# A fused attention and FP4 FFN kernel: FFN units moved beside the second batch, the first fills issued ahead, chunks begun two places later, the last group split

## The chip, the cores and the metric

The kernel runs on one core of one Trainium2 chip. The metric is the device time of one execution in microseconds. Three runs of the kernel before gave 1520.27, 1525.3 and 1527.58 us, median 1525.3. The profile is of one further execution.

## The reference, cut to what matters

```python
# x (8, 256, 512); 16 heads of 16 over C = 256 channels, T = 512 positions
Q, K, V = proj(Wq), proj(Wk), proj(Wv)
att = einsum('bhqd,bhkd->bhqk', Q, K) / sqrt(16) + b[0]
att = softmax(att * m + (1 - m) * NEG_INF)          # m: the mask over keys
y = einsum('bhqk,bhkd->bhqd', att, V) -> (8, 256, 512)
# FFN over the last axis, 512 -> 4096 -> 512, rows are the 2048 (batch, channel) pairs
Wg, Wu, Wd = dequant(4-bit codes, scales of blocks of 32)
out = x + (gelu_tanh(y @ Wg.T) * (y @ Wu.T)) @ Wd.T
```

## The kernel before, in words

**Attention.** Each of the 8 batches goes through four quads of heads. A quad has eight score steps (S00 to S31): two matmuls (line 852) into a pair of PSUM banks, then one exponential over 128 x 1024 on ScalarE (line 633). The product with V (line 866, A0 to A3), a copy (603), a transpose back (873, Y) and a normalisation on VectorE (712, 715, YN) follow, and GpSimd splits the result into two f16 parts y_hi and y_lo (lines 513 and 515). Beside this the maxima of the next quads are found: a step m is a matmul tile (line 836) and a reduction on VectorE, one tile at a time (line 693, batches 0 and 1) or a pair (line 700, later batches). Q, K and V of the next batch are projected in pieces (lines 812 and 822), stored to DRAM (369) and read back as stacks by ten DMAs for each half batch (fill_stack, lines 379 to 384, steps F0, F1 and G1).

**FFN.** The 2048 rows are four chunks of 512 (two batches each). For each chunk the 32 units of 128 hidden columns are gone through: gate (G0 to G3) and up (U0 to U3) are twelve matmuls of 512 columns each (lines 896 to 898, three products of f16 parts), gelu on ScalarE (608), the product inter on VectorE (748), its split into in_hi on ScalarE (615) and in_lo on GpSimd (527). After four units a group's down product (lines 944 to 946) is made for four row tiles r, twelve matmuls each, and VectorE adds it to acc (758).

**Weights.** In chunk 0 each unit's codes are decoded: VectorE unpacks (426, 428, 432), GpSimd multiplies by the scales (400), ScalarE makes the high half (409, weight_hi), VectorE the low half (414, weight_lo). The result is written to DRAM (345, spill_unit) and read again by the later chunks (352). The ring holds eight units. Units 0, 1 and 2 are decoded ahead of chunk 0.

**Order.** All engines walk the same list, written by `schedule()`. Batches below SOLO (0 and 1) use PLAN, with two pairs of score banks and no FFN work. Later batches use SHARED_PLAN, with one pair of score banks (the other two hold gate and up), in which a bar is a place where FFN steps are put: there are 16 in a quad, 64 in a batch. Chunk c begins after step YN of quad 0 of batch 2c + 2, which completes the y of its second batch, and its steps are spread evenly over the places up to the next chunk's start:

```python
ready = [n + 1 for n, (b, g, step, _) in enumerate(steps) if step == "YN" and g == 0 and b >= 2 and b % 2 == 0]
...
count = len(rest) // left
```

Gate of a chunk's first unit waits for y_lo of both batches (line 912). The queues run in order. SP begins with the loads of x[0] and wq, wk, wv, the loads of units 0 and 1 (576 KB each), then seed rows, the stores of Q and K, x[1] and the first fill. ScalarE's queue begins with the masks, among them a broadcast of seven batches' masks to 128 partitions (1.8 MB, line 583), from which VectorE finds any_key (line 723).

Of the kernel before, what the change touches and what calls it, by code (L numbers as in the profile page):

```python
# [6 lines left out]
P = 128  # L7
# [27 lines left out]
STEPS = CHUNKS * UNITS  # L35
# [3 lines left out]
LAST_CHUNK = (CHUNKS - 1) * UNITS  # L39
LAST_SHARED = LAST_CHUNK // GROUP - 1  # L40
SOLO = 2
# [6 lines left out]
def build(nc, x, mask, bias, wq, wk, wv, packed, scales, out):  # L48
# [3 lines left out]
    with ctx:  # L52
# [57 lines left out]
        mask_all = big[:, 0:B * T]  # L110
# [7 lines left out]
        seed = big[0:B, 5632:5632 + 768].bitcast(f16).rearrange("b (r t) -> b r t", r=3)  # L118
        seed_dram = nc.dram_tensor("seed_rows", [B, 3, T], f16, kind="Internal").ap()
# [15 lines left out]
        def out_bank(j, r):  # L135
# [7 lines left out]
        masks_in = sem("masks_in")  # L143
# [121 lines left out]
        def attention():  # L265
# [6 lines left out]
            for step in "| A2 | A3 | AO | | Y | YN".split():  # L272
                yield B, 0, step, None

        def ffn(c):

            for u in range(UNITS * c, UNITS * (c + 1)):
# [6 lines left out]
            if c == CHUNKS - 1:  # L284
                for step in ("G0", "G1"):
                    yield STEPS, step, None
                for r in range(4):
                    for i in range(GROUP):
                        yield STEPS, "D", (STEPS // GROUP - 1, r, i)

        def schedule():
# [3 lines left out]
            ready = [n + 1 for n, (b, g, step, _) in enumerate(steps) if step == "YN" and g == 0 and b >= 2 and b % 2 == 0]  # L295
            for b, g, step, arg in steps[:ready[0]]:
                yield "attention", b, g, step, arg
            for c in range(CHUNKS):
                rest = list(ffn(c))
                span = steps[ready[c]:ready[c + 1]] if c < CHUNKS - 1 else []  # L300
# [22 lines left out]
        def group_free(eng, n):  # L323


            wait_from(eng, sum_mm, 4 * (n // GROUP - 1))
# [20 lines left out]
        def reload_unit(sp, n):  # L347

            group_free(sp, n)
            if n < UNITS + RING:  # L350
# [690 lines left out]
```

## Time and profile before

| | |
|---|---|
| median of three runs | 1525.3 us |
| profiled execution, its time and its span | 1526.61 us, 1524.8 us |
| busy in the span: TensorE, VectorE, ScalarE, GpSimd | 1421.5, 698.3, 752.1, 309.6 us |
| an exponential, a table load, a weight_hi on ScalarE | 1.02, 1.28, 1.48 us |
| an L426 or L428 on VectorE while GpSimd is idle | 0.35 us |
| wait of TensorE for wk at the start | 2.1 us |

The table gives busy times of one execution. Busy time of TensorE is the union of its matmuls as the profile models them. The granted clock is a share of full speed, 1.0 for 2.4 GHz and 0.5 for 1.2 GHz.

### The profile page before, as it was taken

What the parts mean: (1) busy time and instruction counts of PE and PEld (TensorE: products, weight loads), DVE (VectorE), ACT (ScalarE), POOL (GpSimd) and SP (SyncE); (2) the same over time, 40 slices, a digit from 0 to 9 for tenths busy, and PEclk for the clock granted to TensorE, in tenths of its full rate; (3) what the DMA queues carried; (4) which work ended last, traced back from release to release, by engine and by line L of the source; (5) the groups of instructions that cost most, each with busy time, mean ns of one, the idle gap of its engine ahead of it and who ended that gap; (6) DMA issues with size and microseconds to landing.
All of it is one profiled execution on the core that took longest, in us unless ns stands there. A gap on an engine that the chain in (4) does not pass through costs nothing.

```text
span 1524.8 us, 18901 instructions
## 1 busy us (share of the span) xinstructions
PE 1421.5 (93%) x7376; PEld 555.1 (36%) x7376; DVE 698.3 (46%) x934; ACT 752.1 (49%) x855; POOL 309.6 (20%) x242
## 2 busy tenths in 40 slices
PE   3688779999999998999999998999999999999998
PEld 1122223333333333333433333333333334444443
DVE  5667668777778753433344333433343111111111
ACT  2255558666667663555665554556655631111110
POOL 3002024433444421111211111111111111111110
PEclk7589989999999999999999999999999999999999
DMA  5130324443354332432243320432222223233220
GB/s 182 51 87 15 101 78 163 154 131 122 108 183 157 133 125 65 143 99 84 84 128 106 101 84 20 155 119 83 84 84 83 84 83 138 83 126 123 83 84 28
DMA packets 51129, 157.91 MB, mean 104 GB/s; under 512 B 7632, under 2 KB 21072, under 8 KB 50912
## 3 DMA queue, kind: packets, MB, share of 16 engines
q1 hardware_dynamic: 48192, 153.80, 29.5%
q10 hardware_dynamic: 2848, 2.90, 0.6%
q8 instruction: 59, 0.97, 0.3%
q14 instruction: 30, 0.25, 0.1%
HBM read 118.64 MB, written 37.77 MB: 103 GB/s over the span
## 4 chain that ended last, share of the span: by engine, by line
PE 81%; DMA 4%; DVE 3%; ACT 3%; issue 3%; POOL 2%; SPq 2%; ACTq 1%; POOLq 0%; DVEq 0%
PE psum L896 14%; PE psum L897 13%; PE psum L898 13%; PE psum L944 8%; PE psum L945 7%; PE psum L946 7%; PE psum L866 7%; PE psum L852 4%; PE psum L836 4%; PE psum L812 2%; DMA wide<-seed_rows 2%; POOL dq_w L400 1%; DVE w_ring L414 1%; PE psum L822 1%; ACTq L393 1%
## 5 line engine op out<-in xcount | busy, mean ns | idle before, releaser
L633 ACT ACTIVATE big<-psum 128x1024 f32<-128x1024 f32 x256 | 260.1, 1024 | 328.4 <-PE psum L852 321.4
L896 PE MATMUL psum<-y_hi,w_ring 128*128 128x512 f16 x1024 | 390.5, 381 | 16.5 <-POOL y_lo L515 15.8
L898 PE MATMUL psum<-y_hi,w_ring 128*128 128x512 f16 x1024 | 389.6, 380 | 0.0
L897 PE MATMUL psum<-y_lo,w_ring 128*128 128x512 f16 x1024 | 389.4, 380 | 0.0
L700 DVE TENSOR_REDUCE maxima<-psum 128x2 f32<-128x1024 f32 x179 | 219.2, 1225 | 253.6 <-PE psum L836 253.3
L527 POOL TENSOR_TENSOR in_lo<-inter,in_hi 128x512 f16<-128x512 f32 x128 | 150.4, 1175 | 811.1 <-ACT in_hi L615 810.5
L748 DVE SCALAR_TENSOR_TENSOR inter<-psum,gelu 128x512 f32<-128x512 f32 x128 | 88.2, 689 | 315.4 <-PE psum L898 301.4
L944 PE MATMUL psum<-w_ring,in_hi 128*128 128x512 f16 x512 | 195.5, 382 | 7.7 <-ACT gelu L608 4.3
L945 PE MATMUL psum<-w_ring,in_hi 128*128 128x512 f16 x512 | 194.8, 380 | 0.0
L946 PE MATMUL psum<-w_ring,in_lo 128*128 128x512 f16 x512 | 194.6, 380 | 0.0
L896 PEld LDWEIGHTS psum<-y_hi,w_ring 128*128 128x128 f16 x1024 | 100.1, 98 | 202.6 <-issue 82.7
L836 PE MATMUL psum<-wide 51*128 51x512 f16 x512 | 129.0, 408 | 46.4 <-DMA wide<-seed_rows 32.7
L615 ACT CAST in_hi<-inter 128x512 f16<-128x512 f32 x128 | 78.7, 615 | 178.5 <-DVE inter L748 178.4
L758 DVE SCALAR_TENSOR_TENSOR acc<-psum,acc 128x512 f32<-128x512 f32 x128 | 88.5, 691 | 166.0 <-PE psum L946 165.4
L866 PE MATMUL psum<-big,wide 128*32 128x512 f32 x1024 | 140.9, 623 | 7.7 <-DVE y_f L715 6.5
L898 PEld LDWEIGHTS psum<-y_hi,w_ring 128*128 128x128 f16 x1024 | 100.5, 98 | 121.6 <-issue 1.3
L608 ACT ACTIVATE gelu<-psum 128x512 f32<-128x512 f32 x128 | 76.4, 597 | 131.1 <-PE psum L898 130.0
L897 PEld LDWEIGHTS psum<-y_lo,w_ring 128*128 128x128 f16 x1024 | 100.5, 98 | 102.1 <-issue 0.8
L633 ACT ACT_TABLE_LOAD x93 | 119.3, 1283 | 29.9 <-issue 28.6
L400 POOL TENSOR_TENSOR dq_w<-dq_code,dq_scales 128x1536 f32<-128x1536 f16 x32 | 99.8, 3118 | 147.9 <-DVE w_ring L414 122.7
L693 DVE TENSOR_REDUCE maxima<-psum 128x1 f32<-128x512 f32 x154 | 99.5, 685 | 50.4 <-PE psum L836 48.3
L852 PE MATMUL psum<-wide 53*128 53x512 f16 x512 | 111.9, 404 | 10.4 <-DMA wide<-max_lo 8.0
(69 smaller groups left out, 987.3 us busy)
## 6 DMA issues: line engine op xcount, KB each, us to landing
w_ring<-w_parts SPq DMA_DIRECT2D x96, 768.0 KB, 7.2
w_parts<-w_ring SPq DMA_DIRECT2D x32, 768.0 KB, 3.3
dq_scales<-scales SPq DMA_DIRECT2D x32, 384.0 KB
wide<-qk_parts SPq DMA_DIRECT2D x64, 128.0 KB
qk_parts<-wide SPq DMA_DIRECT2D x60, 128.0 KB
dq_packed<-packed SPq DMA_DIRECT2D x32, 192.0 KB
small<-x SPq DMA_DIRECT2D x8, 512.0 KB, 6.6
wide<-qk_parts SPq DMA_DIRECT2D x64, 64.0 KB
```

The lines of the kernel that those rows point to most:

```text
L527: nc.gpsimd.tensor_tensor(in_lo[:, u % IN_RING, :], inter[:, :], in_hi[:, u % IN_RING, :], ALU.subtract).then_inc(in_lo_s, 1)
L633: nc.scalar.activation(p_exp[:, k, :, i], p_score[:, bank:bank + 2, :], ACT.Exp, scale=SCORE_SCALE).then_inc(exp_done, 1)
L700: nc.vector.reduce_max(maxima[:, g % 2, n // 2:n // 2 + 9:8], p_max, AX.X).then_inc(max_red, 2)
L836: nc.tensor.matmul(p_max[:, n % 2, :], q_stack[rows, side, s, t * P:(t + 1) * P], k_stack[rows, side, s, :], start=True, stop=True).then_i ...
L852: last = nc.tensor.matmul(p_score[:, bank + e, :], k_stack[rows, side, s, k * P:(k + 1) * P], q_stack[rows, side, s, :], start=True, stop= ...
L866: last = nc.tensor.matmul(p_av[r:r + 32, :], v_rows[:, k, head_of(g, e, i), :], p_exp[:, k, e, i, :], start=(k == 0), stop=(k == TT - 1))
L896: nc.tensor.matmul(dst, w[:, 0, k % 2, cols], hi, start=(k == 0), stop=False)
L897: nc.tensor.matmul(dst, w[:, 0, k % 2, cols], lo, start=False, stop=False)
L898: return nc.tensor.matmul(dst, w[:, 1, k % 2, cols], hi, start=False, stop=(k == TT - 1))
L944: nc.tensor.matmul(dst, in_hi[:, s, rows], w_hi, start=(i == 0), stop=False)
L945: nc.tensor.matmul(dst, in_hi[:, s, rows], w_lo, start=False, stop=False)
L946: last = nc.tensor.matmul(dst, in_lo[:, s, rows], w_hi, start=False, stop=(i == GROUP - 1))
```

## The change

Visits take the place of units: a visit is a unit, a chunk and a range of the chunk's 512 columns. Units 0 to 7 are first visited with columns 0 to 255 of chunk 0 (batch 0's rows), a segment of its own that begins at batch 1's YN. The second segment holds units 8 to 31 with all 512 columns and then units 0 to 7 again with columns 256 to 511; their weights are read back from DRAM. Matmuls, gelu, inter, in_hi and in_lo of such a visit are 256 wide, and its groups have two row tiles. SOLO goes from 2 to 1, so batch 1 uses SHARED_PLAN, and units 0, 1 and 2 are all decoded in batch 0's plan. The first stack fill is issued before x[1] and the unit loads, the broadcast of seven masks is replaced by a small store and a broadcast of eight numbers. A segment begins at the second place after YN. The down product of the very last group goes unit by unit over the four row tiles.

```diff
+EARLY = 8
+VISITS = ([(n, 0, 0, 256) for n in range(EARLY)] + [(n, 0, 0, 512) for n in range(EARLY, UNITS)]
+          + [(n, 0, 256, 512) for n in range(EARLY)]
+          + [(n, c, 0, 512) for c in range(1, CHUNKS) for n in range(UNITS)])
+STEPS = len(VISITS)
+SEGMENTS = [0, EARLY] + [UNITS * c + EARLY for c in range(1, CHUNKS)] + [STEPS]
+ROWS = [range(VISITS[s][2] // P, VISITS[s][3] // P) for s in range(0, STEPS, 4)]
-SOLO = 2
+SOLO = 1
...
-            "F1 A2 m A3 m AO m S00 S01 V1a m m S10 V1b V1h m S11 m Y S20 MT MH XH YN m m ML S21 MV A0 m m A1 m "
-            "S30 m S31 m Q0a m Q0b m Q0h Q0l",
-            "X A2 m S00 m d0 K0a K0b m K0h S01 m S10 m A3 K0l AO m m S11 Y m MT MH ML S20 MV m S21 m Q1a YN m Q1b "
-            "Q1h m S30 Q1l A0 m m A1 m S31 m",
+            "F1 A2 m A3 m AO m S00 S01 V1a d00 m d01 m d02 S10 V1b V1h m S11 m Y S20 MT MH XH YN m h0 m ML S21 MV A0 l0 m m A1 m "
+            "S30 m S31 m Q0a m Q0b m Q0h Q0l L2",
+            "X A2 m S00 m d10 K0a K0b m K0h S01 d11 m S10 m A3 K0l AO m m S11 Y m MT MH ML S20 MV m S21 m Q1a YN m Q1b "
+            "Q1h m S30 Q1l A0 m d12 m A1 m S31 m",
...
-            for step in "| A2 | A3 | AO | | Y | YN".split():
+            for step in "| A2 | A3 | AO | | Y | YN | |".split():
...
-                for r in range(4):
-                    for i in range(GROUP):
+                for i in range(GROUP):
+                    for r in ROWS[-1]:
                         yield STEPS, "D", (STEPS // GROUP - 1, r, i)
...
+            ready = []
+            for n, (b, g, step, _) in enumerate(steps):
+                if step == "YN" and g == 0 and (b == 1 or b >= 2 and b % 2 == 0):
+                    places = [m for m in range(n, len(steps)) if steps[m][2] == "|"]
+                    ready.append(places[1] + 1)
...
-            load_unit(sp, 0)
-            load_unit(sp, 1)
+            sp.wait_ge(dve_own, 2)
+            sp.dma_start(any_dram, any_b).then_inc(any_out, 16)
             sp.wait_ge(setup, 4)
             sp.wait_ge(fixed, 2)
             sp.dma_start(seed_dram, seed).then_inc(seed_out, 16)
             store_qk(sp, 0, 0, 0)
             store_qk(sp, 0, 0, 1)
+            sp.wait_ge(seed_out, 16)
+            fill_stack(sp, 0, 0, 0, False)
             sp.wait_ge(x_lo_s, 1)
             sp.wait_ge(v_proj, 1)
             load_x(sp, 1)
-            sp.wait_ge(seed_out, 16)
-            fill_stack(sp, 0, 0, 0, False)
+            sp.wait_ge(any_out, 16)
+            sp.dma_start(any_key[:, :], any_dram.rearrange("b o -> (b o)").partition_broadcast(P)).then_inc(any_in, 16)
+            load_unit(sp, 0)
+            load_unit(sp, 1)
             move_max(sp, 0, 0, 0)
...
-            act.dma_start(mask_all[:, T:],
-                          mask[1:].rearrange("b t -> (b t)").partition_broadcast(P)).then_inc(masks_in, 16)
...
-            for n in range(8):
-                reduce_maximum(0, 0, n)
-            weight_lo(dve, 0)
-            for n in range(8, 16):
+            for n in range(16):
                 reduce_maximum(0, 0, n)
...
-                w, c = w_ring[:, u % RING], u // UNITS % 2
+                _, c, first, end = VISITS[u]
+                w, dst = w_ring[:, u % RING], dst[:, first:end]
...
+                u, n = GROUP * j + i, r - ROWS[j][0]
+                if n == 0:
+                    pe.wait_ge(in_lo_s, u + 1)
                 if i == 0:
-                    if r == 0:
-                        pe.wait_ge(in_lo_s, GROUP * j + GROUP)
```

## Rows read from the trace of the kernel before

**Rows 1.** The page: busy time, and the span in 40 slices.

```profile
PE 1421.5 (93%) x7376; PEld 555.1 (36%) x7376; DVE 698.3 (46%) x934; ACT 752.1 (49%) x855; POOL 309.6 (20%) x242
...
PE   3688779999999998999999998999999999999998
...
PEclk7589989999999999999999999999999999999999
```

**Rows 2.** Windows: length, busy us of each engine, granted clock, DMA share, GB/s.

```profile
61.35:138.75 77.40, 60.46 (x346) 16.87 (x345) 49.80 (x86) 39.97 (x48) 8.45 (x8) 0.82 0.24 64
138.75:207.90 69.15, 54.19 (x338) 16.69 (x342) 49.92 (x88) 40.28 (x48) 9.46 (x10) 0.91 0.32 88
...
207.90:221.80 13.90, 7.59 (x58) 3.04 (x51) 8.99 (x12) 5.13 (x7) 3.26 (x3) 0.75 0.14 57
...
371.30:551.30 180.00, 170.60 (x915) 66.36 (x908) 137.70 (x173) 120.79 (x127) 75.89 (x41) 1.00 0.40 135
```

**Rows 3.** Waits of TensorE over the whole span: us, times, longest.

```profile
PE psum L836 <- DMA wide<-seed_rows: 32.7, 4, 17.9
PE psum L896 <- POOL y_lo L515: 15.8, 4, 4.8
```

**Rows 4.** Timeline, start and length: batch 1's start, and the four chunks' first matmuls.

```profile
138.75 0.15 DVE L774 COPY any_now<-any_key 128x1 f32<-128x1 f32 x1
...
221.76 0.61 PE L896 MATMUL psum<-y_hi,w_ring 128*128 128x512 f16 x1 [4.75 <-POOL y_lo L515]
...
576.85 0.39 PE L896 MATMUL psum<-y_hi,w_ring 128*128 128x512 f16 x1 [4.15 <-POOL y_lo L515]
...
924.72 0.39 PE L896 MATMUL psum<-y_hi,w_ring 128*128 128x512 f16 x1 [4.15 <-POOL y_lo L515]
...
1257.87 0.39 PE L896 MATMUL psum<-y_hi,w_ring 128*128 128x512 f16 x1 [2.74 <-POOL y_lo L515]
```

**Rows 5.** Chain and timeline of the first 110 us: start, length, what.

```profile
1.75 11.77 DMA big<-wk
...
26.32 0.40 SPq L333 DMA_DIRECT2D small<-x  x1
...
31.41 0.30 SPq L384 DMA_DIRECT2D wide<-seed_rows  x1
...
40.34 0.61 PE L836 MATMUL psum<-wide 51*128 51x512 f16 x2 [17.89 <-DMA wide<-seed_rows]
...
48.78 1.20 PE L836 MATMUL psum<-wide 51*128 51x512 f16 x2 [1.66 <-DVE maxima L693]
...
102.80 6.53 DMA wide<-seed_rows
```

**Rows 6.** VectorE's groups within batch 3 (371 to 551 us): busy, mean ns, idle before.

```profile
L700 DVE TENSOR_REDUCE maxima<-psum 128x2 f32<-128x1024 f32 x32 | 39.1, 1221 | 10.6 <-PE psum L836 10.4
L414 DVE SCALAR_TENSOR_TENSOR w_ring<-dq_w,w_ring 128x1536 f16<-128x1536 f32 x16 | 28.0, 1751 | 0.0
L428 DVE TENSOR_SCALAR dq_sign<-dq_packed 128x384 uint32<-128x384 uint32 x30 | 19.9, 662 | 0.0
L426 DVE TENSOR_SCALAR dq_code<-dq_packed 128x384 uint32<-128x384 uint32 x30 | 17.1, 569 | 11.0 <-POOL dq_w L400 11.0
L432 DVE TENSOR_TENSOR dq_code<-dq_sign,dq_code 128x768 uint32<-128x768 uint32 x16 | 15.3, 958 | 0.5
```

**Rows 7.** The chain, V's projection of batch 2: start, length.

```profile
193.38 0.78 PE psum L822 x12
```

**Rows 8.** SP's queue: the writing out of units 0, 1 and 2.

```profile
196.67 11.68 SPq L345 DMA_DIRECT2D w_parts<-w_ring  x3
```

**Rows 9.** Timeline of the end: the last group's first matmul and two adds.

```profile
1509.40 0.58 PE L944 MATMUL psum<-w_ring,in_hi 128*128 128x512 f16 x1 [2.72 <-POOL in_lo L527]
...
1516.48 0.69 DVE L758 SCALAR_TENSOR_TENSOR acc<-psum,acc 128x512 f32<-128x512 f32 x1 [1.90 <-PE psum L946]
...
1519.07 0.69 DVE L758 SCALAR_TENSOR_TENSOR acc<-psum,acc 128x512 f32<-128x512 f32 x1 [1.90 <-PE psum L946]
```

More of the change, by code:

```diff
@@ L34 @@
 CHUNKS = B * C // 512
-STEPS = CHUNKS * UNITS
+EARLY = 8
[5 more added lines that the diff above has]
+ROWS = [range(VISITS[s][2] // P, VISITS[s][3] // P) for s in range(0, STEPS, 4)]
+ADD_ORDER = [(j, r) for j, rows in enumerate(ROWS) for r in rows]
+ADD_NO = {key: n + 1 for n, key in enumerate(ADD_ORDER)}
 RING = 2 * GROUP
@@ L294, in schedule @@
             steps = list(attention())
-            ready = [n + 1 for n, (b, g, step, _) in enumerate(steps) if step == "YN" and g == 0 and b >= 2 and b % 2 == 0]
+            ready = []
[3 more added lines that the diff above has]
+                    ready.append(places[1] + 1)
             for b, g, step, arg in steps[:ready[0]]:
                 yield "attention", b, g, step, arg
-            for c in range(CHUNKS):
+            for c in range(len(SEGMENTS) - 1):
                 rest = list(ffn(c))
-                span = steps[ready[c]:ready[c + 1]] if c < CHUNKS - 1 else []
+                span = steps[ready[c]:ready[c + 1]] if c + 1 < len(ready) else []
                 left = sum(step == "|" for _, _, step, _ in span)
@@ L457, in _ @@
                 if kind == "ffn":
-                    u, c = b, b // UNITS
+                    u = b
+                    c = VISITS[u][1] if u < STEPS else CHUNKS
                     if step == "G0" and u < STEPS:
@@ L596, in _ @@
             store_qk(act, 0, 1, 1)
-            weight_hi(act, 0)
             max_part(0, 0, True)
@@ L649, in _ @@
                     x_high(b + 1)
-                elif step == "wh" and b < SOLO:
-                    weight_hi(act, b + 1)
+                elif step in ("h0", "h1", "h2") and b < SOLO:
+                    weight_hi(act, int(step[1]))
         @block.vector
@@ L747, in inter_part @@
                 wait_from(dve, in_lo_s, u)
-                nc.vector.scalar_tensor_tensor(out=inter[:, :], in0=up_bank(u),
+                cols = slice(*VISITS[u][2:])
+                nc.vector.scalar_tensor_tensor(out=inter[:, cols], in0=up_bank(u)[:, cols],
                                                scalar=I_SCALE / (Y_SCALE * W_SCALE),
-                                               in1=gelu[:, u % 2, :], op0=ALU.mult, op1=ALU.mult).then_inc(inter_s, 1)
+                                               in1=gelu[:, u % 2, cols], op0=ALU.mult, op1=ALU.mult).then_inc(inter_s, 1)
             def add_rows(j, r):
-                dve.wait_ge(sum_mm, 4 * j + r + 1)
-                if j % (UNITS // GROUP) == 0:
-                    dve.wait_ge(acc_in, 16 * (j // (UNITS // GROUP)) + 16)
+                dve.wait_ge(sum_mm, ADD_NO[j, r])
+                c = VISITS[GROUP * j][1]
+                earlier = [ADD_NO[m, r] for m in range(j) if VISITS[GROUP * m][1] == c and r in ROWS[m]]
+                if earlier:
+                    dve.wait_ge(acc_add, earlier[-1])
                 else:
-                    dve.wait_ge(acc_add, 4 * (j - 1) + r + 1)
+                    dve.wait_ge(acc_in, 16 * c + 16)
                 nc.vector.scalar_tensor_tensor(out=acc[:, r, :], in0=out_bank(j, r), scalar=1.0 / (I_SCALE * W_SCALE),
@@ L786, in _ @@
                 elif step[0] == "d" and b < SOLO:
-                    decode(dve, b + 1, int(step[1]))
-                elif step == "wl" and b < SOLO:
-                    weight_lo(dve, b + 1)
+                    decode(dve, int(step[1]), int(step[2]))
+                elif step in ("l0", "l1", "l2") and b < SOLO:
+                    weight_lo(dve, int(step[1]))
         @block.tensor
@@ L891, in three_products @@
             def three_products(dst, u, cols, k):
-                w, c = w_ring[:, u % RING], u // UNITS % 2
+                _, c, first, end = VISITS[u]
+                w, dst = w_ring[:, u % RING], dst[:, first:end]
                 cols = slice(cols + k // 2 * P, cols + k // 2 * P + P)
-                hi, lo = (y[:, k, 512 * c:512 * c + 512] for y in (y_hi, y_lo))
+                hi, lo = (y[:, k, 512 * (c % 2) + first:512 * (c % 2) + end] for y in (y_hi, y_lo))
                 nc.tensor.matmul(dst, w[:, 0, k % 2, cols], hi, start=(k == 0), stop=False)
```

92 lines of the change are left out of this document (47 added, 45 removed), and 8 rows, old and new, of the table PLAN.

## The prediction

> **What bounds the kernel now.** I read the page first, then a table of windows, then TensorE's waits, and then the order of time at the two ends. TensorE is busy 93% of the span, and the next engine 49% [rows 1]. The 40 slices show where the other 7% and most of the lost speed lie: the digits of PE are 3, 6, 8, 8, 7 in the first five slices (38 us each) and 9 almost everywhere after that, and the clock row has its low digits there too [rows 1]. The windows say the same in us: batch 0's attention works TensorE 60.5 of 77.4 us at a granted clock of 0.82, batch 1's 54.2 of 69.2 at 0.91, the start of batch 2 7.6 of 13.9 at 0.75, while batch 3, which has FFN units beside it, works it 170.6 of 180.0 at 1.00 [rows 2]. So up to 221.8 us the chain is attention's own (DMA landings, reductions, exponentials), and behind that it is the sum of TensorE's work.
>
> Two prices follow. The last row tiles end 2.59 us apart, 12 matmuls each [rows 9]: 0.216 us for a matmul of 512 columns, 36 of them or 7.77 us for a unit, 248.7 us for a chunk. Chunk 1 begins at 576.85 and chunk 2 at 924.72 [rows 4]: 347.9 us, less the 4.15 us wait at its end 343.7, less 248.7 leaves 95.0, so 47.5 us for one batch of attention and, with 64 places in a batch, 0.74 us of it a place. Chunk 0 took 355.1 us (221.76 to 576.85), 7.2 more.
>
> TensorE's own waits add up to few things: 32.7 us for stacks that land and 15.8 us for y_lo at the four chunk starts [rows 3].
>
> **First fills.** Before, the first stack fill stands in SP's queue behind the load of x[1], which is issued at 26.32 because it waits for x_lo; the last of its ten DMAs goes out at 31.41 and TensorE begins at 40.34, after 17.9 us of waiting [rows 5]. After, the fill stands behind the four stores of Q and K alone. Those waited for K's split; K's matmuls waited for wk, which took 11.8 us from its issue [rows 5] in the company of 1.8 MB of broadcast masks and 1.1 MB of unit loads, both of which go away or go later. I put K's split 2 us earlier (TensorE idled 2.1 us for wk, by the table above), at 15.8; two store issues of 0.6 us each, a landing that I put at 2 to 5 us, ten fill issues as before in 4.9 us, then 6.5 us (the later fill) to 8.9 us (this one) to the first matmul [rows 5]: 30.6 to 35.6. I take 33.3, which is 7 us earlier; bounds 3 and 10. Besides, weight_lo of unit 0 no longer stands between the first sixteen reductions: TensorE waited 1.66 us for it [rows 5]. Start: -8.7 us.
>
> On the queues the trace shows only that big<-wk took 11.8 us while everything else was in flight. The Trainium skill, "DMA: Bandwidth & Descriptors", section "Issuing engines are not separate DMA queues", says that transfers issued by SP and by ACT run on the same sixteen engines; by it the masks on ACT's queue did delay wk, and by the opposite only the unit loads behind wk could have, and the 2 us would be nearer nothing. The trace does not decide it.
>
> **Batch 0.** It now holds the decoding of three units where it held one (unit 0's was in the preamble). One unit costs VectorE two L426, two L428, L432 and L414. Beside attention alone that is 0.35 x 4 (the table above) + 0.96 + 1.75 [rows 6] = 4.1 us, so +8.3 us, and +3.0 us on ScalarE. VectorE is busy 49.8 of these 77.4 us [rows 2] and half of its slack lies between reductions that TensorE waits for in turn. I take half: +4, bounds 0 and +8.3.
>
> **Batch 1 with eight units beside it.** Before, from batch 1's start (138.75) to chunk 0's first matmul (221.76) [rows 4]: 83.0 us. Batch 1 now uses the plan of batches 2 to 7, with one pair of score banks. Its opening up to YN should be like that of batch 2: 13.9 us from batch start to y ready [rows 2]; the two places later fit into what was the 4.75 us wait [rows 4]. Then a batch's length of 64 places with 72 FFN steps, one a place, two in the last eight.
>
> TensorE's work there is 47.5 + 8 x 24 x 0.108 = 20.7 + group 0's two row tiles 5.2 = 73.4 us. VectorE's: 32 pair reductions 39.1; eight decodings at the lengths they have beside GpSimd, 2 x 0.57 + 2 x 0.66 + 0.96 + 1.75 = 5.2, so 41.3 [rows 6]; eight half-width inter at about 0.38, 3.0; two adds 1.4; the remaining pieces of a batch 6.7 (138.75 to 207.9 less reductions and weights): 91.5 us. ScalarE's, by the lengths in the table above: 32 exponentials 32.8, sixteen table loads 20.5, eight weight_hi 11.9, some 14 of small ones: 79 us. VectorE is the longest, so 91.5 is the floor. In-order queues add to it. A unit has four score steps, two places each. Between the first two pairs VectorE has a reduction and four decode pieces, 3.7 us; between the next two a reduction, L432 and weight_lo, 3.9; in the other two it has little, and TensorE's 2.3 us (1.49 attention, 0.65 FFN, 0.16 down) or the exponential's chain rule; I put 2.5 there. 3.7 + 3.9 + 2.5 + 2.5 = 12.6, times 8 = 101 us. Upper bound: batch 1 alone took 69.2 us on 49.9 of VectorE [rows 2], a ratio of 1.38, so 126; this holds 11.3 us of DMA waits that the shared plan should not have.
>
> So 13.9 + 101 = 114.9, +31.9 against 83.0; of this 25.9 us is FFN work that need not be done later, and 2 x 0.74 = 1.5 is batch 2's attention of the two places. Net +4.5, bounds -5 and +29.5.
>
> Is a matmul of 256 columns really half? None is in the trace. Below it, V's projection has twelve of 128 columns, each with its own weights, in 0.78 us or 0.065 each [rows 7]; above it, 512 cost 0.216. So 0.108, with 0.065 and 0.216 as ends; the upper end for 384 such matmuls would cost 41 us, but the 128-column rows exclude it, since they have as many loads and less cover. The Trainium skill, "TensorE: Matmul & The Clock Gate", section "LDWEIGHTS (loading the stationary operand)", has a load cost of columns / 1.2, 107 ns for 128 columns; as a floor for each pair that would leave 256 columns at 0.108 too. Rows 7 go below that floor, so the trace does not bear it out as one.
>
> **Rest of chunk 0.** The restart at 221.76 was cold (a matmul of 0.61 us against 0.39 at the next chunk [rows 4]) and cost about 2; TensorE now comes working. 21 of 29 decodings remain in it: -1. The eight half units at its end have 2.9 steps a place: gelu waits for a table load 1.28, an exponential 1.02 and itself 0.3, 2.6 us, covered by four up steps (1.3) and 1.4 places (1.0): 0.3 to 0.4 us a unit, +3; bounds 0 and +8. Sum 0. The eight further reloads of 768 KB run beside 0.2 to 0.4 of DMA load [rows 2], and three units ahead: nothing; without that cover a reload is 7.2 us.
>
> **Chunks two places later.** The waits at 576.85, 924.72 and 1257.87 were 4.15, 4.15 and 2.74 [rows 4]. Two places hold score and reduction work of 1.5 us and two shares of the previous chunk's FFN (3.9 us each), over 9 us in all. The last chunk too keeps two places. -11.0.
>
> **Last group split.** TensorE stood 2.72 us until in_lo at 1509.40 and began again at half speed (0.58 us for a matmul) [rows 9]. Now 36 of 48 matmuls need only older units and begin where up ends, 1509.40 - 2.72 = 1506.7; 48 x 0.216 = 10.4 ends at 1517.1, against 1521.6 (the last add comes one interval after 1519.07). All four adds and 256 KB stores now come within 2 us, where the last store had the DMA engines to itself: +0.8. -3.7.
>
> Sum: -8.7 + 4 + 4.5 + 0 - 11.0 - 3.7 = -14.9. The profiled execution took 1526.6 us for its span of 1524.8; the median is 1525.3. From the median: 1510.4, rounded 1510.
>
> **Rivals.**
> (A) The eight units drag batch 1. One pair of score banks makes TensorE wait for every exponential, and VectorE's decoding delays each pair reduction, so the stretch takes 126 us as bounded: 1535, slower. It decides from 116 us on (no gain left) and is measurably slower from 124. For it: VectorE would be 91.5 of 101, denser than the 137.7 of 180 of batch 3 [rows 2]. Against: batch 3 shows that decoding and shared banks cost TensorE only 9 us in 180 where work fills in. 0.17.
> (B) The start stays. The first fill's landing, not its place in the queue, is the length, and x and wq are no sooner: 1510 + 7 = 1517. For it: 8.9 us of the 17.9 were landing. 0.12.
> (C) Slack takes it all: batch 0 absorbs the decoding (-4), the stretch runs at VectorE's floor (-9.5), half units don't stall (-3): about 1494. For it: 27.6 us in which VectorE is idle in batch 0 [rows 2]. 0.16.
> (D) The split of the chunk does nothing because batch 1's fills for batch 2 stand behind spills in SP's queue, three of which took 11.7 us to issue [rows 8], and the gaps move to batch 2: +10, 1520. 0.05.
> The forecast itself has 0.5, with 1502 to 1518 as its own range.
>
> **Numbers.** 1510 us, 80% range 1494 to 1531. A change below 0.5% (7.6 us) is about what this measurement can't tell from none. Faster by more: the forecast but for its edge (0.45), C (0.16), half of B (0.05): 0.66. Within: the rest of these, D and a third of A: 0.19. Slower: 0.15.
>
> **What would show it.** In the new profile: the first L836 at 33 and not 40; batch 1's start near 134; first half-width matmul about 14 us later and the first full chunk work near 249; no L896 wait for y_lo; half-width matmuls 0.11 apart; VectorE over 80% busy between; the last down matmuls straight behind the last up. What would make it wrong: above all the length between units 0 and 8.

## The result, and the profile after

The changed kernel took 1542.0 us (median of four runs, 1536.5 to 1543.0) against 1524.3 us for the kernel before, run beside it: a ratio of 1.0106, 95% interval 1.0074 to 1.0138. It is slower by some 16 us; the prediction had 15 us faster. The profiled executions are closer: 1536.5 us for a span of 1534.6 (the fastest of the four), against a span of 1524.8. So the ledger below has 9.8 us to explain against the 14.9 us gain that was forecast, 24.7 us apart.

The page of the changed kernel: busy time, and the first lines of the span in 40 slices (38 us each).

```profile
PE 1423.8 (93%) x7568; PEld 569.3 (37%) x7568; DVE 680.1 (44%) x909; ACT 777.0 (51%) x887; POOL 317.3 (21%) x250
...
PE   3777888898989998999999999999999999999999
...
PEclk7688899999999999999999999999999999999999
```

Against [rows 1] the engines are as busy as before (TensorE 1423.8 for 1421.5), and the clock is below 9 in the first five slices where it was in the first three and the sixth. What is new is 8s in place of 9s in slices 7, 8, 10 and 12, where attention and FFN already run together. (The 8 in slice 16 was there before.)

Windows of the changed kernel: batch 0; batch 1 up to batch 2's start; first half-width matmul to first full-width one; from there to chunk 1. The columns are as in [rows 2].

```profile
53.49:129.67 76.18, 58.42 (x329) 16.15 (x329) 56.84 (x97) 42.24 (x49) 14.65 (x10) 0.85 0.31 80
129.67:226.96 97.29, 79.15 (x513) 30.28 (x511) 68.57 (x92) 64.92 (x75) 26.21 (x20) 0.88 0.40 122
143.96:248.15 104.19, 83.84 (x564) 34.78 (x565) 75.76 (x103) 74.84 (x85) 33.67 (x24) 0.89 0.46 147
248.15:603.35 355.20, 320.36 (x1801) 130.54 (x1799) 217.76 (x286) 225.78 (x244) 121.36 (x72) 0.98 0.38 128
```

The timeline at those places: start, length, what, and in brackets the wait before it.

```profile
24.54 0.32 SPq L400 DMA_DIRECT2D wide<-seed_rows  x1
...
33.77 0.61 PE L851 MATMUL psum<-wide 51*128 51x512 f16 x2 [15.48 <-DMA wide<-seed_rows]
...
143.96 0.39 PE L912 MATMUL psum<-y_hi,w_ring 128*128 128x256 f16 x1 [1.13 <-POOL y_lo L536]
...
151.91 0.27 PE L913 MATMUL psum<-y_lo,w_ring 128*128 128x256 f16 x1
152.02 0.27 PE L914 MATMUL psum<-y_hi,w_ring 128*128 128x256 f16 x1
...
248.15 0.64 PE L912 MATMUL psum<-y_hi,w_ring 128*128 128x512 f16 x1
...
603.35 0.39 PE L912 MATMUL psum<-y_hi,w_ring 128*128 128x512 f16 x1 [1.05 <-POOL y_lo L536]
```

From these starts and those of [rows 2, 4, 5, 9], stage by stage:

| stretch | before | after | difference | predicted |
|---|---|---|---|---|
| up to batch 0's start | 61.35 | 53.49 | -7.9 | -8.7 |
| batch 0 | 77.4 | 76.2 | -1.2 | +4 |
| batch 1's start to first full-width matmul of a chunk | 83.0 | 118.5 | +35.5 | +31.9 |
| from there to chunk 1 | 355.1 | 355.2 | +0.1 | -24.9 |
| chunks 1 to 3 and the end | | | -16.7 | -17.2 |

The prediction gave the two last lines in one sum, -42.1. I divide it by where the work lies. Gate and up of eight half units (20.7) and chunk 1's wait (4.15) leave the fourth line. The half group's down product (5.2) falls in chunk 1, and with it the other waits (6.9), the 1.5 us of attention and the split group (3.7) go into the fifth line.

The fourth line is the surprise. That stretch has lost 20.7 us of TensorE's FFN work and 3.1 us of wait at its end, and is as long as before. Its attention is the same, because its start and its end both moved by two places. Its window in the kernel before (that of the changed kernel is the last one above):

```profile
221.76:576.85 355.09, 336.65 (x1800) 129.51 (x1801) 258.62 (x330) 238.14 (x251) 140.94 (x79) 0.99 0.40 137
```

TensorE is busy 320.4 us for 336.7, which is 16.3 less and not 20.7, at a granted clock of 0.98 for 0.99, and idle 34.8 us for 18.4.

The first line's mechanism is there (the stack fill's last DMA is issued at 24.54 where it was 31.41), and so are the chunks' two places (the y_lo waits are nearly gone) and the split group (13.6 us from the last up-product's reader to the end instead of 18.0).

TensorE's waits over the whole span of the changed kernel: us, times, longest.

```profile
PE psum L867 <- ACT big L654: 23.7, 16, 3.6
PE psum L851 <- DMA wide<-seed_rows: 19.6, 2, 15.5
...
PE psum L912 <- POOL y_lo L536: 2.2, 2, 1.1
```

And between 248 and 603 us alone, the stretch that did not shrink:

```profile
PE psum L851 <- DVE maxima L721: 9.7, 5, 4.0
PE psum L881 <- DVE y_f L736: 9.6, 7, 1.9
PE psum L912 <- ACT gelu L627: 7.3, 5, 2.6
PE psum L961 <- DVE inter L761: 5.1, 4, 1.9
```

y_lo has gone from 15.8 us [rows 3] to 2.2. Of the waits for exponentials (big), 15.4 us lie beside the half-width units. In the stretch there are 31.7 us of waits for maxima, y_f, gelu and inter. (y_f is the normalised attention output; the next quad's product with V writes the bank that it is read from, and so waits for it.) The kernel before has three like them, over its whole span:

```profile
PE psum L866 <- DVE y_f L715: 6.5, 6, 1.1
PE psum L944 <- ACT gelu L608: 4.3, 6, 0.7
PE psum L836 <- DVE maxima L700: 1.2, 1, 1.2
```

That is some 20 us more of waits.

### The profile page after: what moved, and what is told of

Read it like the earlier page. It is cut to its first block, busy times and chain, and to the rows that moved or that the text cites. A ratio compares the mean times of both kernels' runs of the same rounds, so it can differ in the third digit from the quotient of the medians.

```text
span 1534.6 us, 19370 instructions
## 1 busy us (share of the span) xinstructions
PE 1423.8 (93%) x7568; PEld 569.3 (37%) x7568; DVE 680.1 (44%) x909; ACT 777.0 (51%) x887; POOL 317.3 (21%) x250
## 4 chain that ended last, share of the span: by engine, by line
PE 72%; DVE 7%; ACT 6%; DMA 5%; issue 4%; SPq 2%; POOL 2%; ACTq 0%; DVEq 0%; POOLq 0%
PE psum L912 12%; PE psum L914 11%; PE psum L913 11%; PE psum L961 7%; PE psum L963 7%; PE psum L962 7%; PE psum L881 7%; PE psum L867 3%; PE psum L851 3%; DMA dq_scales<-scales 3%; PE psum L827 2%; DVE maxima L721 2%; DVE w_ring L430 2%; POOL dq_w L416 2%; ACT big L654 2%
## 5 line engine op out<-in xcount | busy, mean ns | idle before, releaser
L912 PE MATMUL psum<-y_hi,w_ring 128*128 128x512 f16 (+1 forms) x1088 | 403.4, 371 | 12.7 <-ACT gelu L627 10.5
L913 PE MATMUL psum<-y_lo,w_ring 128*128 128x512 f16 (+1 forms) x1088 | 401.9, 369 | 0.0
L914 PE MATMUL psum<-y_hi,w_ring 128*128 128x512 f16 (+1 forms) x1088 | 401.8, 369 | 0.0
L721 DVE TENSOR_REDUCE maxima<-psum 128x2 f32<-128x1024 f32 x211 | 258.3, 1224 | 231.3 <-PE psum L851 230.5
L548 POOL TENSOR_TENSOR in_lo<-inter,in_hi 128x512 f16<-128x512 f32 (+1 forms) x136 | 149.9, 1102 | 917.5 <-ACT in_hi L636 917.3
L761 DVE SCALAR_TENSOR_TENSOR inter<-psum,gelu 128x512 f32<-128x512 f32 (+1 forms) x136 | 89.4, 657 | 320.1 <-PE psum L914 301.9
L912 PEld LDWEIGHTS psum<-y_hi,w_ring 128*128 128x128 f16 x1088 | 106.6, 98 | 213.3 <-issue 114.7
L636 ACT CAST in_hi<-inter 128x512 f16<-128x512 f32 (+1 forms) x136 | 80.2, 590 | 199.7 <-DVE inter L761 197.8
L881 PE MATMUL psum<-big,wide 128*32 128x512 f32 x1024 | 144.7, 638 | 14.3 <-DVE y_f L736 14.1
L851 PE MATMUL psum<-wide 51*128 51x512 f16 x512 | 119.9, 402 | 39.2 <-DMA wide<-seed_rows 19.6
L914 PEld LDWEIGHTS psum<-y_hi,w_ring 128*128 128x128 f16 x1088 | 107.2, 99 | 116.2 <-issue 1.4
L627 ACT ACTIVATE gelu<-psum 128x512 f32<-128x512 f32 (+1 forms) x136 | 77.8, 572 | 132.3 <-PE psum L914 131.2
L913 PEld LDWEIGHTS psum<-y_lo,w_ring 128*128 128x128 f16 x1088 | 107.1, 98 | 96.4 <-issue 1.6
L627 ACT ACT_TABLE_LOAD x102 | 130.9, 1283 | 1.8
L654 ACT ACT_TABLE_LOAD x101 | 129.6, 1283 | 1.8
```

The lines of the kernel that those rows point to most:

```text
L627: nc.scalar.activation(gelu[:, u % 2, cols], gate_bank(u)[:, cols], ACT.Gelu_apprx_tanh, scale=1.0 / (Y_SCALE * W_SCALE)).then_inc(gelu_s, 1)
L654: nc.scalar.activation(p_exp[:, k, :, i], p_score[:, bank:bank + 2, :], ACT.Exp, scale=SCORE_SCALE).then_inc(exp_done, 1)
L721: nc.vector.reduce_max(maxima[:, g % 2, n // 2:n // 2 + 9:8], p_max, AX.X).then_inc(max_red, 2)
L851: nc.tensor.matmul(p_max[:, n % 2, :], q_stack[rows, side, s, t * P:(t + 1) * P], k_stack[rows, side, s, :], start=True, stop=True).then_i ...
L881: last = nc.tensor.matmul(p_av[r:r + 32, :], v_rows[:, k, head_of(g, e, i), :], p_exp[:, k, e, i, :], start=(k == 0), stop=(k == TT - 1))
L912: nc.tensor.matmul(dst, w[:, 0, k % 2, cols], hi, start=(k == 0), stop=False)
```

## The experiments

Chunk 0 is measured the same way in all of them: from VectorE's first reading of a full-width up product (unit 0's, or unit 8's where there are half-width visits) to chunk 1's first.

**1. No units beside batch 1, and 2. no later places.** The first keeps everything of the change but the eight half-width visits; units 0 to 2 are still decoded in batch 0. The second keeps those visits, and starts every chunk at YN. The diffs are cut to the lines that matter, here and below.

```diff
 e1
-EARLY = 8
-VISITS = ([(n, 0, 0, 256) for n in range(EARLY)] + [(n, 0, 0, 512) for n in range(EARLY, UNITS)]
...
+VISITS = [(n, c, 0, 512) for c in range(CHUNKS) for n in range(UNITS)]
+SEGMENTS = [UNITS * c for c in range(CHUNKS + 1)]
-SOLO = 1
+SOLO = 2
...
 e2
-            for step in "| A2 | A3 | AO | | Y | YN | |".split():
+            for step in "| A2 | A3 | AO | | Y | YN".split():
...
-                    places = [m for m in range(n, len(steps)) if steps[m][2] == "|"]
-                    ready.append(places[1] + 1)
+                    ready.append(n + 1)
```

> The changed kernel without its first part: 32 full units for chunk 0, begun beside batch 2, batch 1 in the plan with two pairs of score banks; early fills, the two later places and the split last group stay. The stages of the changed kernel say: start -8 us, chunk starts -11, tail -4.5, and the loss lies between batch 1's start and chunk 1. Theory A (the two later places, not the eight units, spoil the rest of chunk 0 by moving FFN steps against the attention steps): chunk 0 takes 25 us or more over the 343.7 of its work here too, and the median is 1525 to 1535. Theory B (the loss comes from the eight half-width visits themselves and what they shift): chunk 0 takes 355 or less as before and the median is 1500 to 1506.

> The changed kernel with every segment begun at YN as before, all else as changed. Theory A (phase): the stretch from unit 8's first gate to chunk 1 falls from 355 to 330 us or less, the three chunk starts wait 4.15, 4.15 and 2.7 us again, median 1515 to 1525. Theory B (the half-width visits themselves): the stretch stays at 350 to 360 and the waits at the chunk starts come back, median 1548 to 1554.

The first took 1528.5 us, ratio 1.0018 (1.0003 to 1.0033): the later places, early fills and split group together, forecast at some -20, gave nothing. Chunk 0 lasted 372.6 us where before it was 354.0, chunk 1's start wait included. The second took 1533.6 us, 1.0047 (1.0032 to 1.0062); units 8 onward lasted 347.6 us from the first gate to chunk 1's, of which 6.5 us are chunk 1's start wait: between what the two theories gave. So each of the two edits makes this stretch longer.

**3. Neither: only early fills and the split group.** Both edits above in one kernel.

> Early fills and the split last group alone: no half-width visits, segments begun at YN. By the stages of the changed kernel -8 (start), 0 to -1 (batch 0, which now decodes three units), -4.5 (tail): median 1510 to 1514, chunk 0 in 352 to 358 us. Both theories expect the same; it is the fourth cell of the table, and it shows whether decoding unit 2 in batch 0 instead of batch 1 frees time there (up to -5).

1516.3 us, ratio 0.9934 (0.9919 to 0.9948). Start and end are worth 9 us by the medians, a little less than expected, and chunk 0 is 357.0. The waits beside batch 2's last two quads differ between this kernel and that of experiment 1. The timeline of the kernel of experiment 1:

```profile
293.20 0.38 PE L909 MATMUL psum<-y_hi,w_ring 128*128 128x512 f16 x1 [1.70 <-ACT gelu L624]
...
299.32 1.06 PE L878 MATMUL psum<-big,wide 128*32 128x512 f32 x8 [1.64 <-DVE y_f L733]
...
339.70 0.38 PE L909 MATMUL psum<-y_hi,w_ring 128*128 128x512 f16 x1 [1.21 <-ACT gelu L624]
...
346.26 1.06 PE L878 MATMUL psum<-big,wide 128*32 128x512 f32 x8 [2.08 <-DVE y_f L733]
```

And that of experiment 3:

```profile
296.69 1.07 PE L877 MATMUL psum<-big,wide 128*32 128x512 f32 x8 [1.08 <-DVE y_f L732]
...
301.82 0.38 PE L957 MATMUL psum<-w_ring,in_hi 128*128 128x512 f16 x1 [0.72 <-ACT gelu L623]
...
341.73 1.06 PE L877 MATMUL psum<-big,wide 128*32 128x512 f32 x8 [1.08 <-DVE y_f L732]
...
346.87 0.38 PE L957 MATMUL psum<-w_ring,in_hi 128*128 128x512 f16 x1 [0.73 <-ACT gelu L623]
```

The same places wait in one quad and the next, 47 us apart in the kernel of experiment 1 and 45 in that of experiment 3: a periodic pattern, with another price in each kernel. What makes it periodic stands in the code. After the first places a chunk issues three FFN steps a place, four units with their down product are 4 x 8 + 16 = 48 steps, and a quad is 16 places: 48 again. So FFN and attention meet in the same way in every quad. Which FFN step has just been issued at a named attention step, such as YN, I call the alignment.

**4. Loads behind the spill.** In the changed kernel the scales of three units come late. The trace's chain there (start, length, what):

```profile
338.88 0.30 SPq L400
...
339.63 10.93 DMA dq_scales<-scales
...
350.58 0.04 DVE dq_code L442
```

SP issues a ten-DMA fill up to 339.2 and a unit's codes and scales right behind it, the scales at 339.63. They land after 10.9 us, and VectorE, which decodes them, has waited 7.1. VectorE's waits between 248 and 603 us in the changed kernel:

```profile
DVE dq_code L442 <- DMA dq_scales<-scales: 18.9, 3, 7.1
```

```diff
                     if step == "G0" and u < STEPS:
-                        if u + AHEAD_UNITS + 1 < UNITS:
-                            load_unit(sp, u + AHEAD_UNITS + 1)
+                        if u == 0:
+                            load_unit(sp, AHEAD_UNITS + 1)
...
                             spill_unit(sp, n)
+                        if u + AHEAD_UNITS + 2 < UNITS:
+                            load_unit(sp, u + AHEAD_UNITS + 2)
```

> The changed kernel with one order in SP's queue altered: the load of a unit's codes and scales is issued right behind the spill before it, so that no fill of ten DMAs can stand between. Theory A1 (VectorE waits for late scales three times, 5.9, 7.1 and 5.9 us, because the load stands behind a fill, and the max tiles, inter and normalisation queue up behind it): the three waits go and 15 to 25 us with them, median 1517 to 1527. Theory A2 (the late scales are hidden; it is the order of steps within VectorE's queue that makes TensorE wait for y_f, inter and gelu): at most 5 us, median 1537 to 1542.

1534.1 us, 1.0051 (1.0036 to 1.0067), between the two. The waits for scales are gone, and 8 us by the medians with them; chunk 0 fell by 6.4 us, from 354.3 to 347.9. TensorE's waits for y_f and gelu stayed. So the late scales were a part of the loss, not its cause.

**5 to 7. Where chunk 0 starts.** On experiment 1, chunk 0 alone begins at YN, or five or eight places later.

```diff
+                    later = {2: 0}.get(b, 2)          # e6: 5, e7: 8
-                    ready.append(places[1] + 1)
+                    ready.append(places[later - 1] + 1 if later else n + 1)
```

> Early fills, split last group, and the two later places for chunks 1, 2 and 3 only; chunk 0 begins at YN of batch 2, no half-width visits. Theory A (a group of four units with its down product is 48 steps, at three steps a place sixteen places, which is one quad; so the point at which chunk 0 begins sets, for all eight quads, where decoding falls against YN, and two places later is a bad coincidence): chunk 0 takes 357 us from first inter to first inter as with all chunks at YN, and chunks 1 and 2 keep their gain of 2.9 and 2.2 us: span 1508 to 1511, median 1510 to 1513. Rival C (the loss of 15.6 us has to do with where chunk 0 ends, two places inside batch 4's first quad, beside chunk 1's start): 372 us as with all chunks two places later, median 1523 to 1528.

> As the run before, but chunk 0 begins five places after YN. Theory A: the cost of chunk 0 depends on the place within the quad and not on the delay as such; so it may be above or below 372, and TensorE's waits of 0.6 us and more in chunk 0 recur at the same places of each quad, some 47 us apart, at other steps than with 0 or 2 places. Rival D (each place later costs chunk 0 some 8 us because work beside attention is lost): 390 us or more.

> As before, chunk 0 eight places after YN. Theory A: again a length of its own between 350 and 380 us, periodic waits. Rival D: over 400 us.

Start at YN: 1523.4 us, 0.9984 (0.9966 to 1.0002), chunk 0 367.0 us, with the waits of experiment 1 from the second quad on. Five places later (one execution): chunk 0 370.6 us, the same waits. So the start does not set the pattern; the chunk's end does. The code says why: `count = len(rest) // left` gives two steps a place to the first 16 or so places and then exactly three, counted back from the last place. Moving the end of chunk 0 two places later (chunk 1's start) therefore moves every FFN step of batches 2 and 3 by six steps against attention. Eight places later (one execution), the number of places is small enough for the surplus to fall otherwise, so that the steps stand eight behind instead of six: 359.6 us, although the same work is pressed into fewer places. Rival D, which had 390 us or more and over 400 us for the two, is out.

**8. Thin decoding.** On experiment 1, five decode operations of units 3 to 31 work on 48 of 384 columns.

```diff
+            e = WORDS // 2 if n < AHEAD_UNITS else WORDS // 16
...
-                nc.vector.tensor_tensor(dq_code[:, :, :], dq_sign[:, :, :], dq_code[:, :, :],
+                nc.vector.tensor_tensor(dq_code[:, :, 0:e], dq_sign[:, :, 0:e], dq_code[:, :, 0:e],
```

> No half-width visits, all chunks two places later (as the first experiment), but for units 3 to 31 the five decoding instructions on VectorE work on 48 of 384 columns each, so most of those weights are stale; everything else, its waits too, is in place. Theory A with VectorE's decoding as what collides (normalisation and inter stand behind it in VectorE's queue): the 372.6 us of chunk 0 fall to 350 or less and the waits for y_f and gelu shrink below 5 us together. Rival E (the collision is on ScalarE: weight_hi and table loads before gelu; VectorE is only along for it): waits of gate and down for gelu stay above 10 us, chunk 0 at 362 to 372.

Chunk 0 fell by 13 us to 359.6 (one execution, span 1513.8), between theory A and rival E; y_f's waits fell from 13.7 to 9.8, while those of gate's matmuls for gelu stayed at 9.5, with the same 1.70 and 1.21 in the same places. TensorE's idle time gives 4.9 of the 13 us (27.1 for 32.0). The other 8.1 are its matmuls, busy 332.5 us for 340.6, at a granted clock of 1.00 for 0.98. So VectorE's decoding is a part, and the waits for gelu are another. What stands before such a wait in ScalarE's order its timeline in experiment 1 shows; no run tried it alone:

```profile
285.85 0.62 ACT L633 CAST in_hi<-inter 128x512 f16<-128x512 f32 x1 [3.05 <-DVE inter L758]
...
286.87 0.58 ACT L618 COPY av_sb<-psum 128x512 f32<-128x512 f32 x1
287.46 1.28 ACT L651 ACT_TABLE_LOAD   x1
288.75 1.02 ACT L651 ACTIVATE big<-psum 128x1024 f32<-128x1024 f32 x1
289.67 1.48 ACT L422 ACTIVATE w_ring<-dq_w 128x1536 f16<-128x1536 f32 x1
291.17 1.28 ACT L624 ACT_TABLE_LOAD   x1
292.46 0.60 ACT L624 ACTIVATE gelu<-psum 128x512 f32<-128x512 f32 x1
```

Here ScalarE works without a pause for 7.2 us, from inter's split to the end of the gelu for which gate's matmul at 293.20 (above) waits.

**9, 11, 12. The alignment alone.** On experiment 1 (no half-width visits, two places later), chunk 0's steps are shifted against attention and the rest is left as it is.

```diff
-                    count = len(rest) // left
+                    count = (len(rest) - -6 * (c == 0 and left > 8)) // left      (e9; e11 has -12, e12 has 8)
```

> As the first experiment (no half-width visits, all chunks two places later), but chunk 0's steps are handed out six ahead, up to eight places before its end, so that at every YN of batches 2 and 3 the same FFN step has just been issued as in the kernel before (the last up step of a group's fourth unit) and not six steps less. Theory A': FFN steps go at exactly three a place counted back from the chunk's end, so the end sets the alignment in every quad; with the old alignment chunk 0 takes 355 to 359 us from first inter to first inter instead of 372.6, TensorE waits under 2 us a quad, and the gain at the chunk starts stays: span 1508 to 1512. Rival C' (the two more places at the end cost by themselves, whatever the alignment): 367 to 373 us, span 1520 to 1527.

> As the first of these, but twelve steps ahead, which is six more than in the kernel before: an alignment that none of the kernels had. Theory A': a length of chunk 0 of its own between 350 and 375 us with waits that recur once a quad. The rival that delay as such costs: below the 357 of the old alignment, since FFN steps come sooner.

> No half-width visits, chunk 0's steps handed out eight later still: at every YN of batches 2 and 3 the same step as in the changed kernel (second gate step of a group's third unit). Theory A': chunk 0 takes 375 to 392 us, with the changed kernel's waits once a quad (y_f, max tiles, inter) and VectorE waiting 4 us or more for scales that landed late behind a stack fill. Rival B': nothing like the changed kernel's waits without its half-width visits, 360 to 373 us, no late scales.

With the old alignment back: **1505.2 us (1499.1 to 1508.5), ratio 0.9846 (0.9804 to 0.9888)**, faster than both kernels, chunk 0 349.1 us. Against experiment 1 only the order of the same steps differs, and 23.5 us of chunk 0 go. TensorE's waits from 210 to 575 us in it:

```profile
PE psum L878 <- DVE y_f L733: 8.1, 8, 1.1
PE psum L958 <- ACT gelu L624: 4.3, 6, 0.7
PE psum L909 <- POOL y_lo L533: 2.0, 1, 2.0
PE psum L848 <- DVE maxima L718: 1.2, 1, 1.2
```

Six steps ahead (experiment 11, one execution, 1521.1 us) chunk 0 took 368.4 us. Fourteen steps behind is the alignment that the changed kernel has. Without half-width visits, one execution with it took 1538.8 us, span 1536.9, chunk 0 381.6 us. Its waits from 210 to 600 us are for the same four things as the changed kernel's:

```profile
PE psum L878 <- DVE y_f L733: 13.2, 8, 3.1
PE psum L848 <- DVE maxima L718: 12.8, 8, 4.8
PE psum L909 <- ACT gelu L624: 7.4, 4, 2.6
PE psum L958 <- DVE inter L758: 4.1, 4, 1.2
```

Its timeline shows the late scales too, and a matmul that waits for the reduction behind them:

```profile
461.33 0.36 DVE L439 TENSOR_SCALAR dq_code<-dq_packed 128x384 uint32<-128x384 uint32 x1 [7.70 <-DMA dq_scales<-scales]
...
463.15 0.61 PE L848 MATMUL psum<-wide 51*128 51x512 f16 x2 [3.98 <-DVE maxima L718]
```

Batch 3 lies wholly inside chunk 0, with 64 places and 192 FFN steps in every one of these kernels, so its length can be compared without a correction. Its windows in experiments 9 and 12 (columns as in [rows 2]):

```profile
361.63:541.67 180.04, 170.66 (x915) 66.38 (x908) 137.72 (x174) 120.84 (x127) 75.87 (x41) 1.00 0.40 135
365.68:569.52 203.84, 180.28 (x926) 68.62 (x924) 135.19 (x179) 122.22 (x127) 82.37 (x42) 0.96 0.36 122
```

Of the 23.8 us between them, 14.2 are idle time of TensorE (23.6 for 9.4). The other 9.6 are the same matmuls taking longer, at a granted clock of 0.96 for 1.00. Over the whole of chunk 0 it is 20.7 of idle time and 11.8 of slower matmuls. So a worse alignment comes with a second price beside the waits; that the waits bring the clock down is not shown apart.

**10. The old alignment in the changed kernel.** All of the change stays; the second segment's steps run 14 ahead until ten places before its end.

```diff
+                    count = (len(rest) - -14 * (c == 1 and left > 10)) // left
```

> The changed kernel, complete, with the steps of the segment of units 8 to 31 handed out fourteen ahead until ten places before its end, which gives the alignment of the kernel before. Theory A': of the 355 us from unit 8's first gate to chunk 1 some 20 us go, no late scales, span 1511 to 1517. Rival B' (the eight half-width visits cost by themselves, in that segment too): 345 to 355 us stay, span 1526 to 1535.

1519.2 us, ratio 0.9946 (0.9921 to 0.9971); chunk 0 from unit 8 took 333.1 us instead of 354.3, with no late scales. So 21 us of the change's loss are alignment (15.7 of idle time, 5.5 of slower matmuls), and with it undone the change gains 0.5%. It still lies 14 us above experiment 9.

**13 and 14. What the units beside batch 1 cost.** Experiment 9 with batch 1 on the shared plan but no FFN in it, and experiment 10 with four visits.

```diff
 e13, on e9
-SOLO = 2
+SOLO = 1
 e14, on the changed kernel
-EARLY = 8
+EARLY = 4
+                    count = (len(rest) - -6 * (c == 1 and left > 10)) // left
```

> The fastest version so far (early fills, later places, old alignment, split last group, no half-width visits), but batch 1 goes in the plan with one pair of score banks, without any FFN work or decoding beside it. Batch 1 took 65.6 us from its start to batch 2's start there, and 97.6 with the plan and the eight half-width visits. Theory P (the plan itself costs: every score step waits for the exponential before it): 85 to 95 us here, span 1520 to 1530. Theory V (VectorE's decoding of eight units and the table loads beside it cost): 66 to 75 us, span 1502 to 1511.

> The changed kernel with the old alignment for the second segment, but four half-width visits beside batch 1 instead of eight. Theory P: nearly the whole price is paid for half the work moved: batch 1 at 88 to 96 us, span 1514 to 1520. Theory V: half the price, batch 1 at 80 to 84 us, span 1508 to 1512.

One execution each, spans 1506.9 and 1509.6. Batch 1 took 65.6 us in experiment 9, 75.2 in 13, 81.8 in 14 and 97.6 in 10, so theory V is nearer than P in both. TensorE's longest waits in experiment 13 from 131 to 200 us, and in experiment 10 from its first half-width matmul (147.3) to 248 us:

```profile
PE psum L864 <- ACT big L651: 12.0, 10, 3.6
```

```profile
PE psum L867 <- ACT big L654: 17.5, 11, 2.7
```

Against experiment 9's span of 1501.8 the three are 5.1, 7.8 and 17.7 us longer. But up to batch 1's start all four run the same code, and four executions of experiment 9 lie 9.4 us apart. Counted from batch 1's start to the end, the plan alone costs 4.1 us (1375.5 for 1371.4), four visits 7.2 (1378.6) and eight 15.4 (1386.8). With single executions the first two are not clear of noise. Work is moved forward into batch 1, but there it takes more than it saves.

The table has the kernels by how far their FFN steps stand from those of the kernel before at each quad's YN in batches 2 and 3 (from chunk 0's second quad on), and the length of chunk 0 in us. Kernels whose chunks start at YN have chunk 1's start wait in it (before, e3, e2). Experiments 4 and 8, with the loads or the decoding changed, and 14, with four visits, are left out:

| steps | full-width chunk 0 | with half-width visits |
|---|---|---|
| 0 | before 354.0, e3 357.0, e9 349.1, e13 349.1 | e10 333.1 |
| 6 ahead | e11 368.4 | |
| 6 behind | e1 372.6, e5 367.0, e6 370.6 | |
| 8 behind | e7 359.6 | e2 347.8 |
| 14 behind | e12 381.6 | after 354.3 |

## Why the prediction was wrong, point by point

**Start, -8.7:** right, -7.9. Both parts came: the first maximum at 33.77 where 33 was named, and no wait for unit 0's weight_lo. Rival B, in which the start stays, is out, and wk was not waited for at all: its load took 6.6 us where it took 11.8 [rows 5]. Masks and unit loads both went from beside it, so which of them delayed it is not shown. (The terms behind 33 add up to 30.4 to 35.8, not 30.6 to 35.6; it changes nothing.)

**Batch 0, +4:** -1.2. Its slack took the decoding; here rival C was nearer (no cost at all). One trace can't say more: in the fifteen traces of kernels with this batch 0 it lasted 73.8 to 80.8 us, on average 77.6, against the one 77.4 before.

**Batch 1 with eight units:** +35.5 for +31.9. The parts held: first half-width matmul 14.3 us after batch 1's start for 13.9, and half-width matmuls 0.11 us apart for 0.108. The rest, 104.2 us to the first full-width matmul, was put at 101. That this is so near is in part luck. VectorE's work was put at 91.5 us and over 80%, but it is busy 75.8 of 104.2, 73%, and TensorE's longest wait there is 15.4 us for exponentials, with one pair of score banks. Rival A's mechanism is there, but not at its price of 126. As an edit the step was sized +4.5; experiments 9 and 10 give 15.4 from batch 1's start and 14.1 by medians. Of the 15.4, the stretch from batch 1's start to the first full-width up product makes 12.4 (38.3 us longer for 25.9 moved), the half units at the segment's end 4.6 (put at 3), less 1.6 later. This compares two kernels with the same alignment. The sum against the kernel before is smaller, because batch 1 became shorter by itself in experiment 9, 65.6 for 69.2 us [rows 2].

**Rest of chunk 0, "Sum 0": the step that failed.** It came out at +25.0 (355.2 for 330.2). The step added local prices (a cold restart, fewer decodings, the half units' gelu chain) and took the remaining 24 units' time from before as given. That time depends on which FFN step stands beside which attention step. The change moves it twice. Two later places shift it by six steps, because steps are counted back from the chunk's end. The half-size down product at unit 36, which has 8 steps instead of 16, shifts it by eight more. (The one at unit 8 stands at the front of the list and moves nothing behind it.) The sum of 14 is the worst of the alignments run.

That this is the cause is shown both ways: the alignment alone puts 32.5 us on a kernel without half-width visits (experiments 9 and 12: 349.1 to 381.6), and undone in the changed kernel gives 21.2 back (experiment 10). Of the 25.0 that leaves 3.8, close to the half units' 4.6. Some 6 of the 21 are the late scales (experiment 4, in which the idle time fell from 34.8 to 28.5 us), and 5.5 are matmuls slower at a lower granted clock. The other 9 or so are waits of TensorE for ScalarE and VectorE. Their orders put a table load, an exponential and a weight split ahead of gelu, and decoding ahead of reductions and y_f, as read in the timelines.

**Chunks two places later, -11.0:** the waits went, but not all of it was gained. Without half-width visits (experiment 1) chunk 1 lasted 344.9 us for 347.8 and chunk 2 327.8 for 329.9: 5.0 us for the 6.9 of two waits. At chunk 0 the same edit, by moving its end, cost +15.6 of length (experiment 1 against 3), more than it saves in all. The step priced the wait that it removes and not the order that it shifts.

**Last group split, -3.7:** right, -4.5. In the timeline the last up product is read at 1521.05, and the four last adds begin at 1529.42:

```profile
1521.05 0.69 DVE L761 SCALAR_TENSOR_TENSOR inter<-psum,gelu 128x512 f32<-128x512 f32 x1 [4.49 <-PE psum L914]
...
1529.42 2.63 DVE L773 SCALAR_TENSOR_TENSOR acc<-psum,acc 128x512 f32<-128x512 f32 x4 [7.67 <-PE psum L963]
```

**Rivals.** The time fell outside the range of 1494 to 1531. A, the one on the slow side, named another place. D's place (DMAs that stand behind others in SP's queue) was near what happened to the scales, but it had batch 2's gaps and 10 us. None had alignment. What stays open: why 6 ahead and 6 behind both cost about 20 us was read from waits, not tried engine by engine; experiment 8 shows only what VectorE's decoding does at 6 behind, in one execution. Loads behind the spill together with the old alignment were not run.

## What to carry to other kernels

When two step lists are dealt out into each other by a fixed rule, an edit that moves one end of a list moves every step of it: work out the alignment before and after (which step of the one stands at a named step of the other), and if it changed, put it back or price it, since here it was worth 32 us of 350. A stretch at 90% of TensorE still has that much in its order, because in-order queues turn a late reduction or gelu into a wait in every period. Work moved forward into a stretch bound by other engines pays only if those are idle at the steps that it needs: eight units beside batch 1 cost 14 to 15 us, and the best version run does without them.

## What the runs showed of the hardware

A matmul of 256 columns is issued every 0.11 us with its own weight load (151.91 and 152.02 above), half of the 0.216 of 512 columns. From 143.96 to 248.15 us there are as many weight loads as matmuls (565 and 564), and nothing of the loads shows in the distance.

The granted clock fell where TensorE waited more: over batch 3, with the same work, it was 1.00 with 9.4 us of idle time and 0.96 with 23.6 (experiments 9 and 12), and the matmuls took 170.7 and 180.3 us.

A table load takes 1.28 us, and the ACTIVATE starts 0.01 us behind it (287.46 + 1.28, then 288.75; 291.17 + 1.28, then 292.46). The instruction before each load ends 0.01 to 0.02 us ahead of it (286.87 + 0.58, then 287.46; 289.67 + 1.48, then 291.17). The Trainium skill, "ScalarE: Activation LUTs", section "What ACT_TABLE_LOAD costs", puts a switch at about 2.7 us with the drain and the load itself at about 1283 ns; this trace agrees with the second and shows no drain.

A load of 384 KB (the scales) issued 0.45 us behind the last DMA of a ten-DMA fill landed after 10.9 us, and with the loads moved behind the spill VectorE waited for no scales. The Trainium skill, "DMA: Bandwidth & Descriptors", section "Queues, rings and completion order", has descriptors of one issuing row consumed in ring order on each engine, which would put the scales behind the fill's rows; the two runs agree with it but don't exclude plain contention.
